# Cross attention: key shares projected two steps ahead and evicted behind both exponentials

## The chip, the cores and the metric

One core of one Trainium2 chip runs the program; the metric is the time of one execution in device microseconds (us). A run is one execution, and the figure of a kernel is the median of its runs.

## The reference, cut to what matters

The program is a two-layer Perceiver-like block on 32 sequences of 64 tokens with 256 channels: cross attention, self attention, a mixture of experts, cross attention again, a two-way Mamba and a feed-forward layer. The change touches only the cross attention, which runs twice:

```python
x = x + xattn(layernorm(x), ctx, ctx, Wq, bq, Wk, bk, Wv, bv, Wo, bo)   # and once more without the biases

# B = 32, 64 queries, 1601 keys with 128 channels, 16 heads of 16
qh = heads(q @ Wq + bq); kh = heads(k @ Wk + bk); vh = heads(v @ Wv + bv)
scores = einsum('bhqd,bhkd->bhqk', qh, kh) * scale
attn = softmax(scores)                     # over the 1601 keys of a sequence
out = einsum('bhqk,bhkd->bhqd', attn, vh)  # then @ Wo + bo
```

## The kernel before, in words

`cross_attention` handles one sequence ("batch") `u` after another. The 1601 keys make 13 tiles of 128, taken in pairs, so a batch has `NG` = 7 steps `g` = 0 to 6 (the last has one tile, of 65 keys), and the two calls have 2 x 224 steps. Every engine has its order of work written out by hand over the same 224 steps, and semaphores tie them together.

**A step on TensorE** (`scores`, then the loop from L597) is, in this order: the scores of the step as keys x queries, in halves called LEAD (heads' strips 0, 1) and TRAIL (2, 3), each closed by `lower` (L560), which subtracts the row maximum with one more matmul; among them four matmuls "M" (`largest`, L481), rounded scores of the *next* batch from which VectorE takes the maxima; then "K" (`project_keys`, L468), one of seven shares of the key projection of a later batch; "V" (`project_values`, L499), the values of step `s + 2`; "P" (`weigh`, L531), the weighted sum of step `s - 1`; at `g` = 6 the transposed maxima "T", at `g` = 1 the sums "S", and at `g` = 3 of every second batch the output projection "W". Before the first score, TensorE waits for both exponentials of the step before, which read the same PSUM tile.

**Banks.** M, K, V, P, T, S and W write into four PSUM banks in rotation (`open_bank`): each waits until the operation four places before it in `ORDER` was read out by its reader (ScalarE for K and V, VectorE for the others). The second M matmul of a step so waits for the eviction of K of the step before.

**ScalarE** (from L642): exponential of LEAD (L650), eviction of K to `kT` (`keep_keys`, L624), exponential of TRAIL, eviction of V (`keep_values`, L632).

**GpSimd** (from L686): rounds the share K just evicted to `kT_hi` (`round_keys`, L674; two buffers), and splits the context of batch `u + 2` into high and low parts for the projections (`split_context`: copy L367, subtraction L369), in three pieces `w` = 0, 1, 2 at `g` = 5, 6 and at `g` = 0 of the next batch. K of share `n` and V wait for the low part of their piece (`raw_lo_done`). GpSimd handles the eviction's rounding first, then the piece, in order.

**VectorE** takes four maxima (L712), adds P to the total (`gather`, L749), and at `g` = 2 divides. **SyncE** loads the context of a batch (L442) once the three pieces of the batch before that in its buffer are split.

At step `(u, g)` the share projected is `(u + 1, g + 1)`, at `g` = 6 `(u + 2, 0)`; the M matmuls of step `(u, g)` read share `(u + 1, g)`, so a share is made one step before it is used. The seventh share, number 6, is small (2 x 65 columns).

Of the kernel before, what the change touches and what calls it, by code (L numbers as in the profile page):

```python
# [13 lines left out]
P = 128  # L14
# [6 lines left out]
NB = 512  # L21
# [240 lines left out]
def cross_attention(nc, tag, x_sb, ident, x_sel, pair_mask, ctxT, wq, wk, wv, wo, bq, bv, bo):  # L262
# [15 lines left out]
    def cols(i):  # L278
# [5 lines left out]
    PROLOGUE = (([("C",)] if bo is not None else []) + [("K", 0, 0)]  # L284
                + [op for n in range(NG) for op in ([("K", 0, n + 1)] if n + 1 < NG else [])
                   + [("M", 0, n, j) for j in range(QUADS)]]
                + [("V", 0), ("V", 1), ("K", 1, 0), ("T", 0)])

    def key_share(u, g):

        return (u + 1, g + 1) if g < NG - 1 else (u + 2, 0)

    LEAD = (0, 1)
    TRAIL = (2, 3)
# [28 lines left out]
    with ExitStack() as ctx:  # L323
# [64 lines left out]
            project_queries(nc, inner, tag, x_sb, ident, qT, wq, bq, loads, split_first)  # L388
        qz = sb(f"{tag}_qz", [P, 2, KD, 2, LQ])
        qz_hi = sb(f"{tag}_qz_hi", [P, 2, KD, 2, LQ], F32R)  # L390
        kT_hi = sb(f"{tag}_kT_hi", [P, 2, NB], F32R)
        kT = sb(f"{tag}_kT", [P, 2, KD, LKV])
        v_sb = sb(f"{tag}_v", [P, NG, 2, H, 2 * DH])
        probs = sb(f"{tag}_probs", [P, 2, QUADS, NB])
# [31 lines left out]
        def last_maximum(b, n):  # L426
            return max((("M", b, n, j) for j in range(QUADS)), key=lambda op: AT[op])

        def made(e, op):

            e.wait_ge(misc_ready, AT[op] + 1)
# [15 lines left out]
        def _(pe):  # L447
# [24 lines left out]
            def largest(op):  # L472
                _, b, n, j = op
                dst = open_bank(op)
                pe.wait_ge(kT_hi_done, b * NG + n + 1)
                if n == 0:
                    pe.wait_ge(qz_hi_done, b + 1)
                rows = slice(j * 32, (j + 1) * 32)
                for m, (c, k0, kn) in enumerate(SHARES[n]):
                    kn += kn % 2  # L480
                    ins = nc.tensor.matmul(dst[:, m * kn:(m + 1) * kn], qz_hi[rows, b % 2, c, :, :].rearrange("p s q -> p (s q)"),  # L481
                                           kT_hi[rows, (b * NG + n) % 2, m * kn:(m + 1) * kn], start=True, stop=True)
                ins.then_inc(misc_ready, 1)

            def turn_maxes(op):
                dst = open_bank(op)
                pe.wait_ge(max_done, op[1] + 1)
                for c in range(KD):
                    ins = nc.tensor.transpose(dst[:, c * P:(c + 1) * P],
                                              neg_max[:, c, :, :].rearrange("p j n -> p (j n)"), ident[:, :])  # L490
                ins.then_inc(misc_ready, 1)
# [45 lines left out]
            def scores(s):  # L537
                u, g = divmod(s, NG)
                mine = tiles(g)
                kn = keys(mine[0])  # L540
                parts = [(h, c) for h in range(len(mine)) for c in range(KD)]
                if g == 0:
                    pe.wait_ge(qz_done, u + 1)
                if s > 0:
                    pe.wait_ge(exp_done, 2 * s)
                if g == 0:
                    read_out(pe, ("T", u))
                last = u + 1 == B

                def score(n, strips):  # L550
                    h, c = parts[n]
                    for j in strips:
                        rows = slice(j * 32, (j + 1) * 32)
                        nc.tensor.matmul(score_ps[0:kn, j, n * P:(n + 1) * P], kT[rows, u % 2, c, cols(mine[h])],  # L554
                                         qz[rows, u % 2, c, :, :].rearrange("p s q -> p (s q)"),
                                         start=n == 0, stop=False, skip_group_check=True)

                def lower(strips):
                    for j in strips:
                        nc.tensor.matmul(  # L560
                            score_ps[0:kn, j, 0:len(mine) * 2 * P], ones[j * 32:j * 32 + 1, 0:kn],
                            shift[j * 32:j * 32 + 1, u % 2, :].rearrange("p (a n) -> p a n", a=1
                                                                         ).broadcast_to([1, len(mine), 2 * P]),
                            start=False, stop=True, skip_group_check=True).then_inc(score_ready[j // 2], 1)

                for n in range(2):
                    score(n, LEAD)
                if not last:
                    for j in TRAIL:
                        largest(("M", u + 1, g, j))  # L570
                for n in range(len(parts)):
                    score(n, TRAIL)
                    if n + 2 < len(parts):
                        score(n + 2, LEAD)
                    elif n + 2 == len(parts):
                        lower(LEAD)
                if not last:
                    for j in LEAD:
                        largest(("M", u + 1, g, j))
                lower(TRAIL)  # L580
# [12 lines left out]
            project_values(("V", 0))  # L593
            project_values(("V", 1))
            project_keys(("K", 1, 0))
            turn_maxes(("T", 0))
            for s in range(STEPS):  # L597
                u, g = divmod(s, NG)
# [17 lines left out]
        @block.scalar  # L616
        def _(act):
            def keep_keys(op):
                _, b, n = op
                made(act, op)  # L620
                c, k0, kn = SHARES[n][0]
                m = len(SHARES[n])
                even = kn + kn % 2
                nc.scalar.activation(kT[:, b % 2, c:c + m, k0:k0 + kn],  # L624
                                     bank(op)[:, 0:m * even].rearrange("p (c k) -> p c k", c=m)[:, :, 0:kn], ACT.Copy
                                     ).then_inc(act_free, 1)

            def keep_values(op):
                g = op[1] % NG
                rows, n = slice(0, keys(tiles(g)[0])), len(tiles(g))  # L630
                made(act, op)
                nc.scalar.activation(  # L632
                    v_sb[rows, g, 0:n, :, 0:DH].rearrange("p a h d -> p (a h) d"),
                    bank(op)[rows, 0:n * D].rearrange("p (a d) -> p a d", d=DH), ACT.Copy).then_inc(act_free, 1)

            act.wait_ge(filled, 1)
            for n in range(NG):
                keep_keys(("K", 0, n))
            keep_values(("V", 0))
            keep_values(("V", 1))  # L640
            keep_keys(("K", 1, 0))
            for s in range(STEPS):  # L642
                u, g = divmod(s, NG)
                rows, n = slice(0, keys(tiles(g)[0])), len(tiles(g)) * 2 * P
                if s > 1:
                    made(act, ("P", s - 2))
                for ph in range(2):
                    js = slice(2 * ph, 2 * ph + 2)
                    act.wait_ge(score_ready[ph], 2 * s + 2)
                    nc.scalar.activation(probs[rows, s % 2, js, 0:n], score_ps[rows, js, 0:n], ACT.Exp).then_inc(exp_done, 1)  # L650
                    if ph == 0 and key_share(u, g)[0] < B:
                        keep_keys(("K",) + key_share(u, g))
                if s + 2 < STEPS:
                    keep_values(("V", s + 2))

        @block.gpsimd
        def _(pool):
# [7 lines left out]
            def round_keys(b, n):  # L665

                at = b * NG + n
                if at > 1:
                    made(pool, last_maximum(*divmod(at - 2, NG)))
                read_out(pool, ("K", b, n))  # L670
                c, k0, kn = SHARES[n][0]
                m = len(SHARES[n])
                even = kn + kn % 2
                nc.gpsimd.tensor_copy(kT_hi[:, at % 2, 0:m * even].rearrange("p (c k) -> p c k", c=m)[:, :, 0:kn],  # L674
                                      kT[:, b % 2, c:c + m, k0:k0 + kn]).then_inc(kT_hi_done, 1)

            pool.wait_ge(w_in, 16 * NW)
# [5 lines left out]
            for b in range(2):  # L683
                queries(b, qz, qz_done)
            round_keys(1, 0)
            for s in range(STEPS):  # L686
                u, g = divmod(s, NG)
                if key_share(u, g)[0] < B:
                    round_keys(*key_share(u, g))
                if g == 0 and 1 < u + 1 < B:  # L690
                    split_context(pool, u + 1, 2)
                if g == 2 and 1 < u + 1 < B:
                    pool.wait_ge(exp_done, 2 * u * NG)
                    queries(u + 1, qz, qz_done)
                if g == 3 and u + 2 < B:
                    made(pool, last_maximum(u, NG - 1))
                    queries(u + 2, qz_hi, qz_hi_done)
                if g == 5 and u + 2 < B:
                    made(pool, ("V", u * NG + NG - 1))
                    split_context(pool, u + 2, 0)  # L700
                if g == 6 and u + 2 < B:
                    split_context(pool, u + 2, 1)

        @block.vector
        def _(dve):
# [1483 lines left out]
```

## Time and profile before

| | |
|---|---|
| median of 3 runs | 4214.39 us (4214.13 to 4221.18) |
| the profiled execution | 4220.17 us, span in the profile 4218.4 us |
| busy share of the span | TensorE matmul 87%, weight load 62%, VectorE 67%, ScalarE 47%, GpSimd 36% |
| load of a batch's context (L442 and the first two), 64 of 800.5 KB | median 4.3 us to landing |

The steps of the first call fill the span from 86 to 1097 us, those of the second from 1929 to 2944 us; what lies between and behind is untouched by the change. A row of a timeline gives the start in us from the span's start, the duration in us, engine, line, operation, tiles, shape and how many instructions were merged; in brackets stands the idle time before it and what ended it.

### The profile page before, as it was taken

What the parts mean: (1) busy time and instruction counts of PE and PEld (TensorE: products, weight loads), DVE (VectorE), ACT (ScalarE), POOL (GpSimd) and SP (SyncE); (2) the same over time, 40 slices, a digit from 0 to 9 for tenths busy, and PEclk for the clock granted to TensorE, in tenths of its full rate; (3) what the DMA queues carried; (4) which work ended last, traced back from release to release, by engine and by line L of the source; (5) the groups of instructions that cost most, each with busy time, mean ns of one, the idle gap of its engine ahead of it and who ended that gap; (6) DMA issues with size and microseconds to landing.
All of it is one profiled execution on the core that took longest, in us unless ns stands there. A gap on an engine that the chain in (4) does not pass through costs nothing. (4 is left out here: it accounts for less than half of the span.)

```text
span 4218.4 us, 129595 instructions
## 1 busy us (share of the span) xinstructions
PE 3654.6 (87%) x54334; PEld 2636.2 (62%) x54335; DVE 2813.2 (67%) x4793; ACT 1986.8 (47%) x2986; POOL 1523.2 (36%) x1445
## 2 busy tenths in 40 slices
PE   6999999999797299939999999999778778787888
PEld 4888888888687266627888888887323333332357
DVE  5667667666466122236666666665979999999964
ACT  2666666666333122205666666665444444444432
POOL 3333333333000200042333333332067777788710
PEclk8999999999898599968999999999889998999989
DMA  2000001000001501020000100100022222222200
GB/s 64 27 30 31 27 27 34 27 27 19 9 0 56 208 28 32 30 79 25 27 27 27 34 27 27 34 27 3 27 67 70 70 69 71 73 78 73 70 29 20
DMA packets 79936, 182.53 MB, mean 43 GB/s; under 512 B 10754, under 2 KB 31266, under 8 KB 79042
## 3 DMA queue, kind: packets, MB, share of 16 engines
q1 hardware_dynamic: 76354, 166.58, 12.7%
q8 instruction: 413, 6.77, 0.7%
q0 software_dynamic: 3072, 8.39, 0.6%
q14 instruction: 97, 0.79, 0.1%
HBM read 157.37 MB, written 17.56 MB: 41 GB/s over the span
## 5 line engine op out<-in xcount | busy, mean ns | idle before, releaser
L650 ACT ACTIVATE x_probs<-x_score_ps 128x1024 f32<-128x1024 f32 (+1 forms) x896 | 861.0, 963 | 648.3 <-PE x_score_ps L560 641.3
L712 DVE TENSOR_REDUCE x_maxes<-x_misc_ps 128x1 f32<-128x512 f32 (+1 forms) x1792 | 1010.4, 626 | 145.6 <-PE x_misc_ps L481 145.2
L674 POOL CAST x_kT_hi<-x_kT 128x512 fp32r<-128x512 f32 (+1 forms) x448 | 259.5, 579 | 1360.6 <-PE x_misc_ps L499 836.8
L1706 PE MATMUL b_acc_ps<-b_read,ident 128*128 128x512 f32 x1024 | 564.9, 681 | 190.5 <-POOL b_read L1792 157.0
L1784 POOL TENSOR_TENSOR b_drive<-b_b_all,b_dtx 128x1024 f32<-128x1024 f32 x256 | 603.1, 2357 | 331.1 <-DVE b_dtx L1864 281.1
L554 PE MATMUL x_score_ps<-x_qz,x_kT 32*128 32x128 f32 x13312 | 641.0, 277 | 43.3 <-ACT x_probs L650 38.3
L554 PEld LDWEIGHTS x_score_ps<-x_qz,x_kT 32*128 32x128 f32 x13312 | 551.6, 182 | 117.3 <-ACT x_probs L650 60.5
L1826 DVE TENSOR_TENSOR_SCAN b_state<-b_decay_ps,b_drive 128x512 f32<-128x512 f32 x512 | 607.0, 1205 | 12.5 <-POOL b_drive L1784 12.5
L1774 ACT ACTIVATE b_decay_ps<-b_dt,b_a_neg 128x504 f32<-128x504 f32 x512 | 350.0, 685 | 461.9 <-DVE b_state L1826 461.9
L1706 PEld LDWEIGHTS b_acc_ps<-b_read,ident 128*128 128x128 f32 x1024 | 193.8, 211 | 507.7 <-POOL b_read L1792 260.1
L531 PE MATMUL x_misc_ps<-x_probs,x_v 128*32 128x64 f32 x26624 | 464.6, 221 | 0.5 <-issue 0.5
L481 PE MATMUL x_misc_ps<-x_kT_hi,x_qz_hi 32*128 32x512 f32 (+1 forms) x2048 | 452.9, 403 | 5.0 <-POOL x_kT_hi L674 3.0
L531 PEld LDWEIGHTS x_misc_ps<-x_probs,x_v 128*32 128x32 f32 x26624 | 392.3, 110 | 66.4 <-issue 18.2
L749 DVE TENSOR_TENSOR x_u<-x_misc_ps,x_u 128x256 f32<-128x256 f32 x384 | 162.5, 423 | 308.7 <-PE x_misc_ps L531 308.6
L560 PE MATMUL x_score_ps<-x_shift,x_ones 1*128 1x512 f32 (+1 forms) x1792 | 367.1, 459 | 0.3 <-issue 0.3
L624 ACT ACTIVATE x_kT<-x_misc_ps 128x512 f32<-128x512 f32 (+1 forms) x448 | 248.2, 554 | 207.0 <-PE x_misc_ps L468 194.1
L632 ACT ACTIVATE x_v<-x_misc_ps 128x512 f32<-128x512 f32 (+1 forms) x448 | 255.9, 571 | 12.4 <-PE x_misc_ps L499 12.3
L1836 DVE TENSOR_TENSOR b_read<-b_c_ps,b_state 128x512 f32<-128x512 f32 x384 | 254.0, 661 | 0.0
L468 PE MATMUL x_misc_ps<-x_raw_hi,x_wk_hi 128*128 128x512 f32 (+1 forms) x512 | 230.9, 451 | 24.0 <-POOL x_v L680 8.9
L481 PEld LDWEIGHTS x_misc_ps<-x_kT_hi,x_qz_hi 32*128 32x128 f32 x2048 | 235.5, 186 | 24.7 <-DVE x_u L749 8.8
L499 PE MATMUL x_misc_ps<-x_wv_hi,x_raw_hi 128*128 128x256 f32 (+1 forms) x832 | 241.3, 290 | 0.1
L369 POOL TENSOR_TENSOR x_raw_lo<-x_raw,x_raw_hi 128x512 fp32r<-128x512 f32 (+1 forms) x192 | 235.3, 1225 | 15.5
(282 smaller groups left out, 5816.1 us busy)
## 6 DMA issues: line engine op xcount, KB each, us to landing
x_raw<-in_ctxT SPq DMA_DIRECT2D x64, 800.5 KB, 4.3
b_b_all<-b_bc_rows SPq DMA_DIRECT2D x128, 256.0 KB, 3.5
b_c_all<-b_bc_rows SPq DMA_DIRECT2D x128, 256.0 KB, 3.2
m_w<-in_m_w SPq DMA_DIRECT2D x16, 704.0 KB, 19.1
m_w<-in_m_w SPq DMA_DIRECT2D x8, 768.0 KB, 19.6
m_slot_rows<-m_zero SPq DMA_DIRECT2D x1, 4992.0 KB, 17.1
m_block_rows<-m_slot_rows SPq DMA_DIRECT2D x39, 128.0 KB, 2.0
m_slot_out<-m_out SPq DMA_DIRECT2D x39, 128.0 KB, 1.7
```

What stands on the lines that cost most here:

```text
L481: ins = nc.tensor.matmul(dst[:, m * kn:(m + 1) * kn], qz_hi[rows, b % 2, c, :, :].rearrange("p s q -> p (s q)"), kT_hi[rows, (b * NG + n) ...
L531: ins = nc.tensor.matmul(dst[j * 32:(j + 1) * 32, r * LQ:(r + 1) * LQ], v_sb[0:keys(i), g, h, 8 * c + 2 * j + half, :], probs[0:keys(i), s ...
L554: nc.tensor.matmul(score_ps[0:kn, j, n * P:(n + 1) * P], kT[rows, u % 2, c, cols(mine[h])], qz[rows, u % 2, c, :, :].rearrange("p s q -> p ...
L560: nc.tensor.matmul(score_ps[0:kn, j, 0:len(mine) * 2 * P], ones[j * 32:j * 32 + 1, 0:kn], shift[j * 32:j * 32 + 1, u % 2, :].rearrange("p ...
L632: nc.scalar.activation(v_sb[rows, g, 0:n, :, 0:DH].rearrange("p a h d -> p (a h) d"), bank(op)[rows, 0:n * D].rearrange("p (a d) -> p a d" ...
L650: nc.scalar.activation(probs[rows, s % 2, js, 0:n], score_ps[rows, js, 0:n], ACT.Exp).then_inc(exp_done, 1)
L674: nc.gpsimd.tensor_copy(kT_hi[:, at % 2, 0:m * even].rearrange("p (c k) -> p c k", c=m)[:, :, 0:kn], kT[:, b % 2, c:c + m, k0:k0 + kn]).th ...
L712: nc.vector.tensor_reduce(maxes[:, c:c + m, j, k0 // NB], bank(op)[:, 0:m * even].rearrange("p (c k) -> p c k", c=m)[:, :, 0:kn], AX.X, AL ...
L1706: nc.tensor.matmul(acc_ps[:, c, :], ident[:, :], read[:, c, :], start=False, stop=True, skip_group_check=True).then_inc(acc_done, 1)
L1774: nc.scalar.activation(by_sequence(decay_ps[:, c % 2, :])[:, :, inside(p)], by_sequence(dt[:, c, :])[:, :, inside(p)], ACT.Exp, scale=a_ne ...
L1784: nc.gpsimd.tensor_tensor(drive[:, c:c + 2, :], b_all[:, k % 2:k % 2 + 1, :].broadcast_to([P, 2, NB]), dtx[:, c:c + 2, :], ALU.mult).then_ ...
L1826: nc.vector.tensor_tensor_scan(order(state[:, c, :]), order(decay_ps[:, c % 2, :]), order(drive[:, c, :]), 0.0, ALU.mult, ALU.add).then_in ...
```

## The change

- The share of step `(u, g)` becomes `(u + 1, g + 2)`, at `g` = 5 and 6 `(u + 2, 0)` and `(u + 2, 1)`; one more share is made ahead of the loop. `kT_hi` gets a third buffer.
- ScalarE evicts K behind both exponentials.
- TensorE waits for the first exponential alone ahead of the LEAD scores, and for the second ahead of the TRAIL scores.
- GpSimd splits the pieces `w` = 0, 1, 2 at `g` = 4, 5, 6, each one step earlier.

```diff
-                + [("V", 0), ("V", 1), ("K", 1, 0), ("T", 0)])
+                + [("V", 0), ("V", 1), ("K", 1, 0), ("K", 1, 1), ("T", 0)])
     def key_share(u, g):
-        return (u + 1, g + 1) if g < NG - 1 else (u + 2, 0)
+        return (u + 1 + (g + 2) // NG, (g + 2) % NG)
...
-        kT_hi = sb(f"{tag}_kT_hi", [P, 2, NB], F32R)
+        kT_hi = sb(f"{tag}_kT_hi", [P, 3, NB], F32R)
...
-                                           kT_hi[rows, (b * NG + n) % 2, m * kn:(m + 1) * kn], start=True, stop=True)
+                                           kT_hi[rows, (b * NG + n) % 3, m * kn:(m + 1) * kn], start=True, stop=True)
...
                 if s > 0:
-                    pe.wait_ge(exp_done, 2 * s)
+                    pe.wait_ge(exp_done, 2 * s - 1)
...
                 if not last:
                     for j in TRAIL:
                         largest(("M", u + 1, g, j))
+                if s > 0:
+                    pe.wait_ge(exp_done, 2 * s)
                 for n in range(len(parts)):
                     score(n, TRAIL)
...
             project_keys(("K", 1, 0))
+            project_keys(("K", 1, 1))
...
             keep_keys(("K", 1, 0))
+            keep_keys(("K", 1, 1))
...
-                    if ph == 0 and key_share(u, g)[0] < B:
-                        keep_keys(("K",) + key_share(u, g))
+                if key_share(u, g)[0] < B:
+                    keep_keys(("K",) + key_share(u, g))
                 if s + 2 < STEPS:
                     keep_values(("V", s + 2))
...
-                if at > 1:
-                    made(pool, last_maximum(*divmod(at - 2, NG)))
+                if at > 2:
+                    made(pool, last_maximum(*divmod(at - 3, NG)))
...
             round_keys(1, 0)
+            round_keys(1, 1)
             for s in range(STEPS):
                 u, g = divmod(s, NG)
                 if key_share(u, g)[0] < B:
                     round_keys(*key_share(u, g))
-                if g == 0 and 1 < u + 1 < B:
-                    split_context(pool, u + 1, 2)
...
-                if g == 5 and u + 2 < B:
-                    made(pool, ("V", u * NG + NG - 1))
-                    split_context(pool, u + 2, 0)
-                if g == 6 and u + 2 < B:
-                    split_context(pool, u + 2, 1)
+                w = g - (NG - WIDE)
+                if w >= 0 and u + 2 < B:
+                    made(pool, ("V", u * NG + (2 * w + 1 if w < WIDE - 1 else NG - 1)))
+                    split_context(pool, u + 2, w)
```

## Rows read from the trace of the kernel before

**Rows 1.** Busy time by stretch: the first call's steps (columns in the first line)
```profile
core 0: us, PE busy (x) PEld busy (x) DVE busy (x) ACT busy (x) POOL busy (x), PEclk, DMA share, GB/s
86.00:1097.00 1011.00, 982.49 (x24046) 821.07 (x24047) 682.04 (x1261) 628.58 (x887) 320.93 (x457) 1.00 0.08 26
```

**Rows 2.** Waits: who waited for what, us in total, times, longest
```profile
PEld x_misc_ps L468 <- DVE x_maxes L712: 120.0, 425, 0.8
...
PEld x_score_ps L554 <- ACT x_probs L650: 60.5, 135, 1.1
```

**Rows 3.** The tile of the low context part: who waited for it, us, times
```profile
  PE x_misc_ps L468: 6.0, 31
```

**Rows 4.** Timeline of PE, batch 10 from its step 2, into batch 11
```profile
413.93 0.50 PE L468 MATMUL x_misc_ps<-x_raw_hi,x_wk_hi 128*128 128x512 f32 x1
...
415.52 1.10 PE L531 MATMUL x_misc_ps<-x_probs,x_v 128*32 128x64 f32 x64
416.55 0.38 PE L554 MATMUL x_score_ps<-x_qz,x_kT 32*128 32x128 f32 x2
...
423.26 0.38 PE L554 MATMUL x_score_ps<-x_qz,x_kT 32*128 32x128 f32 x2
...
424.84 0.50 PE L468 MATMUL x_misc_ps<-x_raw_hi,x_wk_hi 128*128 128x512 f32 x1
...
426.08 1.10 PE L531 MATMUL x_misc_ps<-x_probs,x_v 128*32 128x64 f32 x64
427.40 0.38 PE L554 MATMUL x_score_ps<-x_qz,x_kT 32*128 32x128 f32 x2 [0.22 <-ACT x_probs L650]
...
429.17 0.30 PE L468 MATMUL x_misc_ps<-x_raw_hi,x_wk_hi 128*128 128x66 f32 x1
...
431.78 0.33 PE L554 MATMUL x_score_ps<-x_qz,x_kT 32*65 32x128 f32 x2
...
432.84 0.50 PE L468 MATMUL x_misc_ps<-x_raw_hi,x_wk_hi 128*128 128x512 f32 x1
...
435.71 0.38 PE L554 MATMUL x_score_ps<-x_qz,x_kT 32*128 32x128 f32 x2
...
438.89 0.65 PE L531 MATMUL x_misc_ps<-x_probs,x_v 65*32 65x64 f32 x32
439.85 0.38 PE L554 MATMUL x_score_ps<-x_qz,x_kT 32*128 32x128 f32 x2 [0.31 <-ACT x_probs L650]
...
441.89 0.47 PE L468 MATMUL x_misc_ps<-x_raw_hi,x_wk_hi 128*128 128x512 f32 x1 [0.20 <-POOL x_raw_lo L369]
```

**Rows 5.** Timeline of ACT: steps 4, 5, 6 of batch 10; then the last batch
```profile
424.77 1.02 ACT L650 ACTIVATE x_probs<-x_score_ps 128x1024 f32<-128x1024 f32 x1 [3.07 <-PE x_score_ps L560]
...
430.06 0.28 ACT L624 ACTIVATE x_kT<-x_misc_ps 128x130 f32<-128x130 f32 x1
...
433.85 0.60 ACT L624 ACTIVATE x_kT<-x_misc_ps 128x512 f32<-128x512 f32 x1 [0.56 <-PE x_misc_ps L468]
...
1078.39 1.94 ACT L650 ACTIVATE x_probs<-x_score_ps 128x1024 f32<-128x1024 f32 x2 [1.08 <-PE x_score_ps L560]
1080.21 0.60 ACT L632 ACTIVATE x_v<-x_misc_ps 128x512 f32<-128x512 f32 x1
```

**Rows 6.** Timeline of POOL: the low parts of one batch, and one piece of another
```profile
431.42 1.27 POOL L369 TENSOR_TENSOR x_raw_lo<-x_raw,x_raw_hi 128x512 fp32r<-128x512 f32 x1
...
435.83 1.28 POOL L369 TENSOR_TENSOR x_raw_lo<-x_raw,x_raw_hi 128x512 fp32r<-128x512 f32 x1
...
440.33 1.42 POOL L369 TENSOR_TENSOR x_raw_lo<-x_raw,x_raw_hi 128x577 fp32r<-128x577 f32 x1
...
590.98 1.09 POOL L369 TENSOR_TENSOR x_raw_lo<-x_raw,x_raw_hi 128x512 fp32r<-128x512 f32 x1
```

**Rows 7.** Timeline of PE in the last batch, step 1
```profile
1076.87 1.16 PE L554 MATMUL x_score_ps<-x_qz,x_kT 32*128 32x128 f32 x30 [0.51 <-ACT x_probs L650]
...
1079.21 1.10 PE L531 MATMUL x_misc_ps<-x_probs,x_v 128*32 128x64 f32 x64
```

More of the change, by code:

```diff
@@ L673, in round_keys @@
                 even = kn + kn % 2
-                nc.gpsimd.tensor_copy(kT_hi[:, at % 2, 0:m * even].rearrange("p (c k) -> p c k", c=m)[:, :, 0:kn],
+                nc.gpsimd.tensor_copy(kT_hi[:, at % 3, 0:m * even].rearrange("p (c k) -> p c k", c=m)[:, :, 0:kn],
                                       kT[:, b % 2, c:c + m, k0:k0 + kn]).then_inc(kT_hi_done, 1)
```

## The prediction, made before the change was run

> **What bounds the kernel now.** I read the busy times by stretch first. In the steps of a call TensorE's matmul rows are busy 982.49 of 1011 us at a granted clock of 1.00 (2.4 GHz), ScalarE 629, VectorE 682, GpSimd 321 [rows 1]: TensorE's queue sets the pace, and another engine costs time only where that queue stands still for it. The waits say where it does. Over both calls it is 120.0 us, in 425 steps, ahead of K for VectorE's maxima, which the change leaves alone, and 60.5 us, 135 times, at the first score for the exponentials, which is the change's target [rows 2]. For GpSimd's low context parts the matmuls stood only 6.0 us, 31 times [rows 3].
>
> The timeline shows these waits in single steps. Where nothing waits, the next step's first score starts 1.03 us behind the start of P (415.52 to 416.55), 0.07 before P's end [rows 4]. Step 4 of batch 10 has P at 426.08, so step 5 could start at 427.11; it starts at 427.40, late by 0.29, released by the exponential. Step 0 of batch 11 has its short P at 438.89, ends it at 439.54, could hand over at 439.47, and does at 439.85: late by 0.38. In the other steps P ends last. So a batch holds some 0.67 us of this wait in two steps, and 62 batches some 42 us of the 60.5.
>
> **The chain that I follow.** GpSimd rounds the evicted keys, then splits a context piece, and K of the next step needs that piece. The pieces move one step earlier, and so do the shares that read them: the distance between them stays one step. But GpSimd's step begins with the key eviction, and that moves behind the second exponential. All times below are from the start of the named step.
>
> *ScalarE.* The first exponential starts 1.51 in (424.77 less 423.26) [rows 4, 5]. Two exponentials back to back hold the next instruction back by 1.82 (1078.39 to 1080.21) [rows 5], so the eviction starts at 3.33. Before, the small one in step 5 started at 2.66 (430.06 less 427.40). By the Trainium skill (ScalarE: Activation LUTs, section What ACT_TABLE_LOAD costs) an activation of N elements takes 186 ns plus 0.833 ns each and back-to-back ones overlap by about 93 ns. That is an estimate of 0.95 us of spacing where the trace has 0.91, and by it each late piece below would be 0.07 later, some 8 us in all.
>
> *Step 4, now with the small share.* Its length loses the 0.29 and nothing else, since a small K and a large one take alike from K to the next step (429.17 to 431.78 is 2.61, 413.93 to 416.55 is 2.62 [rows 4]): 3.85. From the small eviction to the subtraction's start is 1.36 (430.06 to 431.42), the subtraction takes 1.27, in alternate batches 1.09 [rows 5, 6], and K follows its end by 0.15 (432.69 to 432.84; 441.75 to 441.89) [rows 4, 6]. The piece so lets K go at 3.33 + 1.36 + 1.27 + 0.15 = 6.11, or 5.93. K of step 5 would want to go at 3.85 + 1.58 = 5.43 (1.58 is 424.84 less 423.26). **It stands 0.68 or 0.50 us.** Step 6 starts 2.62 later, at 8.73 or 8.55, where before it started at 8.52.
>
> *Step 5.* Its eviction starts at 3.85 + 3.33 = 7.18. A full share has 1.98 from eviction to subtraction (433.85 to 435.83) [rows 5, 6]: K of step 6 can go at 7.18 + 1.98 + 1.28 + 0.15 = 10.59, or 10.40. It would want to at 8.73 + 1.06 = 9.79 or 9.61 (432.84 less 431.78) [rows 4]. **It stands 0.80 us.** From there to the next batch is 2.87 (432.84 to 435.71): 13.46 or 13.27, against 12.45 before (423.26 to 435.71). These three steps lose 1.01 or 0.82.
>
> *Step 6.* Its K is late, so its eviction comes 1.01 behind that K (432.84 to 433.85). I estimate the subtraction of the widest piece to start 2.04 behind it, 0.06 more than for a full one, and take it at 1.42, or some 0.2 less [rows 6]. K of step 0 can go 1.01 + 2.04 + 1.42 + 0.15 = 4.62 (or 4.4) behind the late K, and would want to at 2.87 + 1.58 = 4.45: late by 0.17, or not at all.
>
> *Steps 0 and 1.* The wait of 0.38 goes; with the 0.17 that leaves 0.21 in alternate batches. What is late next is the bank: the second M matmul of step 1 waits for the eviction of step 0, which now ends at 3.33 + 0.60 = 3.93. With 0.05 for the release, an estimate below GpSimd's 0.15, I put M at 3.98, where it would want to go near 3.78: 0.2 lost in one kind of batch, little in the other. Before, K of step 1 went at 2.04 in batch 11 (441.89 less 439.85), held by the widest piece, and I estimate 1.84 where the pieces are 0.2 shorter. Now it goes at 1.58 plus what M lost. So step 1 gains some 0.40 in the batches with long pieces and 0.05 in the others.
>
> *The sum.* Long pieces: +1.01 - 0.21 - 0.40 = +0.40. Short pieces: +0.82 - 0.38 - 0.05 = +0.39. I take +0.395 for each of the 60 batches whose steps split a piece (30 in a call): +23.7 us. The next to last batch splits nothing and gains some 0.5; the last one has no M and no K, and both exponentials end last there: those from 1078.39 end at 1080.33 and would let go at 1080.38, P from 1079.21 would hand over at 1080.24 [rows 5, 7]. That is 0.14 in each of five steps, and the first, with its short P, has near the whole 0.51 of idle time: some 1.2. Twice 1.7 is -3.4. Together **+20 us**.
>
> *Costed at nothing.* The extra share ahead of the loop is taken from step 6 of the next to last batch. The third buffer only loosens a wait. The new wait ahead of the TRAIL scores holds those and all behind them, but its exponential ends at 1.51 + 0.91 + 1.02 = 3.44, before any next step starts. The context load of SyncE is released one step earlier with the widest piece, takes 4.3 us, and is needed four steps later. Rounding has two steps for its share instead of one. If GpSimd's pieces were not late, these covers would still stand.
>
> The profiled execution took 4220.17 us, 5.8 above the median of 4214.39. From it I get 4240; as a median of runs, 4214.4 + 20 = **4234**.
>
> **Rivals.**
> *Faster: the pieces come in time.* Place: the K of steps 5 and 6. It decides at 5.43 after the start of step 4: were the low part done by 5.28, nothing would stand. For it speaks that GpSimd is idle two thirds of the time [rows 1] and that it did just this before [rows 3]. Against it, GpSimd's queue is in order with the eviction at its head, and the sum misses by 0.50 at least. Then the three steps take 3.85 + 4.20 + 3.93 = 11.98 instead of 12.45, and a batch gains 0.47 + 0.38 + 0.15 = 1.00: 60 times, with the 3.4, -63 us, 4151. By the Trainium skill (Perfetto Trace Analysis, section Identifying the Most-Contended Engine) TensorE's headroom is judged by its weight loads, here 821 of 1011 us or 81% [rows 1]. That would leave it room to gain from every wait removed; the waits for exponentials in the trace are 60.5 us in all [rows 2].
> *No difference.* The late pieces cost what the exponentials give: one of the two stands, say the 0.80 halved. A batch then breaks even: about 4214.
> *Slower by more.* The bank wait of M in step 1 also takes the overlap of M with the scores. Step 5 began behind a wait and had its K at 1.77 instead of 1.58 [rows 4]. If step 1 does so in each batch, 0.19 x 60 is 11 more, and 4245; with longer subtractions when they lie beside the moved eviction, 4256.
> *The change doesn't do what it says*: the first scores can't start earlier, since P sits before them. That is so in five steps of seven already; its chance is counted with the case of no difference.
>
> **How the numbers follow.** Forecast (4222 to 4245) 0.50; faster by the pieces in time or mostly so 0.20; no difference 0.15; slower by more 0.15. Within 0.2% (8.4 us, about what a measurement can tell) falls 0.18 and above it 0.62 (0.03 of the forecast lies within). The range from 4185 to 4256 takes in the break-even and half of the way to the faster case, and leaves the full -63 out. Its bounds cover the subtraction of 1.09 to 1.28 and the skipped 0.2 of M.
>
> **What would show it.** Right: the wait of the first score for the exponential is nearly gone; K's wait for the low part rises from 6 us to some 70 to 90; step 4 shrinks to 3.85, steps 5 and 6 take 4.7 to 4.9; the key eviction starts at 3.33. Wrong: K in step 5 before 5.9 from the start of step 4, or no wait for L369; then the faster case holds. M in step 1 at 3.8 would show no bank wait.

## The result and the profile after

The changed kernel takes 4227.42 us (median of 9 runs, 4224.98 to 4230.58), the kernel before 4215.44 us in the same comparison. The ratio is 1.0028, 95% interval 1.0017 to 1.0038: slower by 12.0 us. The forecast was 4234, slower by 20.

The profiled execution took 4226.03 us, with a span of 4224.3. The busy times of the first call's steps (columns as in [rows 1]), which now end at 1101 instead of 1097 us:

```profile
86.00:1101.00 1015.00, 966.38 (x24015) 806.13 (x24013) 686.82 (x1260) 615.10 (x886) 317.72 (x455) 1.00 0.08 26
```

TensorE's matmul rows fell from 982.49 to 966.38 us while the stretch grew by 4: TensorE stands idle for longer. The granted clock is 1.00 as before. The waits of the changed kernel (who waited for what, us in total, times, longest) say for what:

```profile
PEld x_misc_ps L468 <- DVE x_maxes L714: 190.4, 407, 1.1
...
PE x_misc_ps L468 <- POOL x_raw_lo L369: 67.6, 93, 1.1
...
PEld x_score_ps L554 <- ACT x_probs L654: 0.6, 2, 0.3
```

The wait of the first score for an exponential is gone, 60.5 to 0.6 us [rows 2]. In its place K waits for the low context parts, 67.6 us where it was 6.0 [rows 3]. The row above it, up from 120.0 to 190.4 [rows 2], is partly the same wait: K waits for VectorE's maximum and for the low part in one place, and the profile books the idle time of the weight loads to one name and that of the matmuls to the other. The run e1 below decides it: with the low parts in time the 190.4 fall to 103.6.

The timeline of PE shows the steps 4, 5 and 6 of batch 12, one of those whose pieces take GpSimd 1.27 us ("long", against 1.09):

```profile
488.29 0.38 PE L554 MATMUL x_score_ps<-x_qz,x_kT 32*128 32x128 f32 x2
...
489.87 0.30 PE L468 MATMUL x_misc_ps<-x_raw_hi,x_wk_hi 128*128 128x66 f32 x1
...
492.06 0.38 PE L554 MATMUL x_score_ps<-x_qz,x_kT 32*128 32x128 f32 x2
...
494.39 0.47 PE L468 MATMUL x_misc_ps<-x_raw_hi,x_wk_hi 128*128 128x512 f32 x1 [0.68 <-POOL x_raw_lo L369]
...
497.00 0.33 PE L554 MATMUL x_score_ps<-x_qz,x_kT 32*65 32x128 f32 x2
...
498.80 0.48 PE L468 MATMUL x_misc_ps<-x_raw_hi,x_wk_hi 128*128 128x512 f32 x1 [0.78 <-POOL x_raw_lo L369]
...
501.62 0.38 PE L554 MATMUL x_score_ps<-x_qz,x_kT 32*128 32x128 f32 x2
```

Timelines of ACT and of POOL in the same steps:

```profile
489.81 1.94 ACT L654 ACTIVATE x_probs<-x_score_ps 128x1024 f32<-128x1024 f32 x2 [3.77 <-PE x_score_ps L560]
491.63 0.29 ACT L627 ACTIVATE x_kT<-x_misc_ps 128x130 f32<-128x130 f32 x1
```
```profile
492.05 0.29 POOL L678 CAST x_kT_hi<-x_kT 128x130 fp32r<-128x130 f32 x1 [5.38 <-ACT x_kT L627]
492.28 0.61 POOL L367 CAST x_raw_hi<-x_raw 128x512 fp32r<-128x512 f32 x1
492.98 1.27 POOL L369 TENSOR_TENSOR x_raw_lo<-x_raw,x_raw_hi 128x512 fp32r<-128x512 f32 x1
...
497.38 1.27 POOL L369 TENSOR_TENSOR x_raw_lo<-x_raw,x_raw_hi 128x512 fp32r<-128x512 f32 x1
```

Read as one chain: the exponentials start 1.52 after the step and hold the eviction until 3.34 (491.63). GpSimd, idle for 5.38 us, rounds and only then splits, the low part is done at 494.25, and K follows at 494.39, which is 6.10 after the start of step 4. Step 4 is 3.77 long, step 5 4.94, step 6 4.62: 13.33 together, where they were 12.45 [rows 4].

Step 1 shows the wait for the bank. The timeline of PE at the start of the steps 0 and 1 of the same batch has the second M matmul of step 1 at 472.40, 0.24 behind the start of its step:

```profile
468.40 0.38 PE L554 MATMUL x_score_ps<-x_qz,x_kT 32*128 32x128 f32 x2
...
472.16 0.38 PE L554 MATMUL x_score_ps<-x_qz,x_kT 32*128 32x128 f32 x2
472.18 0.49 PE L481 MATMUL x_misc_ps<-x_kT_hi,x_qz_hi 32*128 32x512 f32 x1
...
472.40 0.50 PE L481 MATMUL x_misc_ps<-x_kT_hi,x_qz_hi 32*128 32x512 f32 x1
```

The key eviction of step 0, which that bank waits for, ends at 472.35 (timeline of ACT):

```profile
471.74 0.61 ACT L627 ACTIVATE x_kT<-x_misc_ps 128x512 f32<-128x512 f32 x1
```

One step is longer and was not on the list, step 3: 6.89 us in the even batches, which project the output there, where it was 6.71, and in the odd ones 4.95 where it was 4.77. Its K starts 2.34 after the step's start (483.74), before it was 2.16. VectorE's division in step 2 is the way to the cause. The group of its product (L733 before, L735 now), first the row of the kernel before, then that of the changed one; columns busy us and mean ns, then the idle time before it:

```profile
L733 DVE TENSOR_TENSOR x_oT<-x_u,x_recip 128x256 f32<-128x256 f32 x64 | 27.2, 424 | 2.2
```
```profile
L735 DVE TENSOR_TENSOR x_oT<-x_u,x_recip 128x256 f32<-128x256 f32 x64 | 37.9, 592 | 2.2
```

The same instruction takes 0.17 us more in each batch. Timelines of POOL and DVE of the changed kernel, step 2 of batch 12:

```profile
481.86 0.61 POOL L663 TENSOR_TENSOR x_qz<-x_qT,x_mask 128x256 f32<-128x256 f32 x1
```
```profile
482.15 0.60 DVE L735 TENSOR_TENSOR x_oT<-x_u,x_recip 128x256 f32<-128x256 f32 x1
482.67 0.41 DVE L751 TENSOR_TENSOR x_u<-x_misc_ps,x_u 128x256 f32<-128x256 f32 x1
```

GpSimd's masked queries now lie beside the product. In the same step of the kernel before (timelines of POOL and DVE) they had ended before the product began:

```profile
480.40 0.63 POOL L659 TENSOR_TENSOR x_qz<-x_qT,x_mask 128x256 f32<-128x256 f32 x1
```
```profile
481.47 0.42 DVE L733 TENSOR_TENSOR x_oT<-x_u,x_recip 128x256 f32<-128x256 f32 x1
```

They started 3.88 us into their step and now start 4.65 into it: moving the key eviction moved them 0.8 us later. Behind the product stands `gather` (L751), which frees the bank that an M matmul of step 3 waits for, and behind that one stands K.

### The profile page after: what moved, and what is told of

It reads as the page before. It is cut to its first block and busy times, and to the rows that moved or that the text cites. A ratio compares the mean times of both kernels' runs of the same rounds, so it can differ in the third digit from the quotient of the medians.

```text
span 4224.3 us, 129713 instructions
## 1 busy us (share of the span) xinstructions
PE 3622.3 (86%) x54334; PEld 2605.3 (62%) x54335; DVE 2823.5 (67%) x4793; ACT 1962.3 (46%) x2986; POOL 1518.5 (36%) x1445
## 5 line engine op out<-in xcount | busy, mean ns | idle before, releaser
L654 ACT ACTIVATE x_probs<-x_score_ps 128x1024 f32<-128x1024 f32 (+1 forms) x896 | 814.3, 960 | 739.0 <-PE x_score_ps L560 729.8
L554 PE MATMUL x_score_ps<-x_qz,x_kT 32*128 32x128 f32 x13312 | 614.5, 277 | 1.4 <-DVE x_shift L724 1.2
L554 PEld LDWEIGHTS x_score_ps<-x_qz,x_kT 32*128 32x128 f32 x13312 | 525.1, 182 | 65.4 <-issue 32.1
L751 DVE TENSOR_TENSOR x_u<-x_misc_ps,x_u 128x256 f32<-128x256 f32 x384 | 162.2, 422 | 321.6 <-PE x_misc_ps L531 321.6
L560 PE MATMUL x_score_ps<-x_shift,x_ones 1*128 1x512 f32 (+1 forms) x1792 | 348.4, 458 | 0.3 <-issue 0.3
L468 PE MATMUL x_misc_ps<-x_raw_hi,x_wk_hi 128*128 128x512 f32 (+1 forms) x512 | 227.5, 444 | 99.3 <-POOL x_raw_lo L369 67.6
L481 PEld LDWEIGHTS x_misc_ps<-x_kT_hi,x_qz_hi 32*128 32x128 f32 x2048 | 216.5, 186 | 45.5 <-DVE x_u L751 29.7
L369 POOL TENSOR_TENSOR x_raw_lo<-x_raw,x_raw_hi 128x512 fp32r<-128x512 f32 (+1 forms) x192 | 234.6, 1222 | 15.5
```

Of the source, the lines that this page charges most:

```text
L560: nc.tensor.matmul(score_ps[0:kn, j, 0:len(mine) * 2 * P], ones[j * 32:j * 32 + 1, 0:kn], shift[j * 32:j * 32 + 1, u % 2, :].rearrange("p ...
```

## The experiments

e1 to e4 are edits of the changed kernel and share the runs of the kernel before (4215.08 us).

**e1: the split ahead of the rounding.**

```diff
 for s in range(STEPS):
     u, g = divmod(s, NG)
+    w = g - (NG - WIDE)
+    if w >= 0 and u + 2 < B:
+        made(pool, ("V", u * NG + (2 * w + 1 if w < WIDE - 1 else NG - 1)))
+        split_context(pool, u + 2, w)
     if key_share(u, g)[0] < B:
         round_keys(*key_share(u, g))
...
-    w = g - (NG - WIDE)
...
-        split_context(pool, u + 2, w)
```

> Edit to the changed kernel: GpSimd splits the context piece ahead of rounding the share, so the split no longer stands behind the key eviction. Theory 1 (the pieces are late only because the eviction is ahead of them in GpSimd's queue): the low part is done some 3 us before K wants it, K of steps 5, 6 and 0 stops waiting for it (67.6 us in the profile of the changed kernel falls to about 0), step 5 goes from 4.94 or 4.73 to 4.20, step 6 from 4.63 to about 3.9, and a batch loses 1.46 or 1.27: about -82 us against 4227, so 4145, ratio to the kernel before 0.983. Rival (GpSimd's own speed, or another wait behind it, holds K): steps 5 and 6 stay above 4.5 and the time above 4200.

Measured: 4149.38 us, ratio 0.9842 (0.9827 to 0.9857). Timeline of PE in the same three steps of batch 12:

```profile
479.67 0.38 PE L554 MATMUL x_score_ps<-x_qz,x_kT 32*128 32x128 f32 x2
...
481.26 0.50 PE L468 MATMUL x_misc_ps<-x_raw_hi,x_wk_hi 128*128 128x512 f32 x1
...
483.88 0.33 PE L554 MATMUL x_score_ps<-x_qz,x_kT 32*65 32x128 f32 x2
...
484.94 0.50 PE L468 MATMUL x_misc_ps<-x_raw_hi,x_wk_hi 128*128 128x512 f32 x1
...
487.81 0.38 PE L554 MATMUL x_score_ps<-x_qz,x_kT 32*128 32x128 f32 x2
```

Step 5 is 4.21 long, step 6 3.93, and no K waits for L369 any more: that row is gone from the waits. The low part for K of step 5 was done at 476.17, before its step began:

```profile
474.90 1.27 POOL L369 TENSOR_TENSOR x_raw_lo<-x_raw,x_raw_hi 128x512 fp32r<-128x512 f32 x1
```

GpSimd does the same work at the same speed; only its order changed. The place in the queue made the pieces late, and the lateness cost 78 us.

**e2: the queries one step earlier.**

```diff
-                if g == 2 and 1 < u + 1 < B:
+                if g == 1 and 1 < u + 1 < B:
                     pool.wait_ge(exp_done, 2 * u * NG)
                     queries(u + 1, qz, qz_done)
```

> Edit to the changed kernel: GpSimd makes the masked queries of the next batch at step 1 instead of step 2. Theory 2 (in step 2 the moved GpSimd work lies beside VectorE's product of two SBUF operands, L735, which takes 0.60 instead of 0.42 us, and its delay passes through gather and the bank of M to K of step 3): the product is back at 0.42, K of step 3 goes from 2.32 back to 2.15 after the step's start, -0.18 in each of 62 batches, -11 us: about 4216, ratio 1.000. Rival (step 3 is longer for another reason, such as the longer steps before): K of step 3 stays at 2.32 and the time at 4227.

Measured: 4215.26 us, ratio 0.9999 (0.9990 to 1.0008). From the timelines of POOL, DVE and PE, batch 12:

```profile
476.90 0.61 POOL L663 TENSOR_TENSOR x_qz<-x_qT,x_mask 128x256 f32<-128x256 f32 x1
```
```profile
482.22 0.42 DVE L735 TENSOR_TENSOR x_oT<-x_u,x_recip 128x256 f32<-128x256 f32 x1
```
```profile
481.48 0.38 PE L554 MATMUL x_score_ps<-x_qz,x_kT 32*128 32x128 f32 x2
...
483.63 0.50 PE L468 MATMUL x_misc_ps<-x_raw_hi,x_wk_hi 128*128 128x512 f32 x1
```

The product is back at 0.42 and K of step 3 at 2.15. The 12 us are as large as the whole loss of the change: without this overlap the change would have come out even.

**e3: both.**

> Both edits together. If theories 1 and 2 are both right and independent, the gains add: 4227 - 82 - 11 = 4134, ratio 0.981. If the pieces, now early in GpSimd's step, lie beside VectorE's work and slow it, less: 4145 or above.

Measured: 4139.29 us, ratio 0.9819 (0.9804 to 0.9834). The two gains add: 88 us against 78 + 12 = 90.

**e4: the wait for both exponentials back ahead of the first score.**

```diff
-                    pe.wait_ge(exp_done, 2 * s - 1)
+                    pe.wait_ge(exp_done, 2 * s)
```

> Edit to the changed kernel: TensorE waits for both exponentials ahead of the first score again. Theory 3 (the halved wait is worth nothing where P sits before the scores, since with the eviction behind them both exponentials end 3.46 after the step's start and the next step starts at 3.75 at the earliest): steps 0 to 6 stay as they are, and only the steps of the last batch and the first step of the first, now 2.9 to 3.4 long, go back to 3.51, some 1.5 us a call: about 4230, ratio 1.0035. Rival (the halved wait is what removes the wait at steps 0 and 4): these go back up by 0.3 to 0.4 each, +40 us, 4267.

Measured: 4228.97 us, ratio 1.0034 (1.0022 to 1.0046), where the changed kernel has 1.0028. In the changed kernel the halved wait is worth nothing that can be told: the moved eviction alone lets the exponentials end before P. In the traces only the edges of a call show it: the last batch takes 21.57 us from the start of its first step to that of its last, where the changed kernel takes 20.03.

e5 to e8 share 4216.38 us of the kernel before; e5 to e7 are edits of that kernel.

**e5: the halved wait alone.** As in the change, `2 * s - 1` ahead of the first score and `2 * s` ahead of the TRAIL scores.

> Edit to the kernel before: the halved wait alone (first exponential ahead of the LEAD scores, second ahead of the TRAIL scores); eviction, shares and splits as before. Theory 3 goes on: with the eviction between them the second exponential ends 4.10 after the step's start, and the TRAIL scores want to start near 3.95, so the wait of 0.38 at step 0 shrinks to some 0.2. K of step 1 is held by the widest context piece anyway (it goes at 5.97 or 6.18 after the start of step 0), so nothing comes of it there; step 4 may give 0.1 to 0.3. 62 times that, and some 2 in the last batches: -8 to -20 us, about 4202, ratio 0.997. Rival (the halved wait removes both waits in full): -0.67 x 62 = -42, 4173, ratio 0.990.

Measured: 4194.86 us, ratio 0.9953 (0.9939 to 0.9967). That is a little beyond the expected range. This one part of the change is a gain by itself. Its trace places it in step 4, which goes from 4.15 to 3.86 us (even batches, medians). At step 0 the whole wait goes, 4.14 to 3.76, and not half of it as expected, but step 1 loses as much, 5.06 to 5.43: its K is held by the widest context piece and goes 5.96 us after the start of step 0 either way.

**e6: the eviction alone.**

```diff
-                    if ph == 0 and key_share(u, g)[0] < B:
-                        keep_keys(("K",) + key_share(u, g))
+                if key_share(u, g)[0] < B:
+                    keep_keys(("K",) + key_share(u, g))
```

> Edit to the kernel before: the key eviction moved behind both exponentials, nothing else. GpSimd's rounding then starts 4.08 after the step's start and ends at 4.69, and the first M of the next step, which reads it, can go at 4.84 instead of 3.8 to 4.2: three steps of a batch lose 1.0, 0.6 and 1.0, and the late context pieces some 1.3 more, less the 1.2 of waits that the eviction removes: about +168 us, 4380, ratio 1.04. That would show why the shares had to go two steps ahead. Rival (rounding has slack enough in its one step): the time stays within 20 us of the kernel before.

Measured: 4352.83 us (one run), 136 above the kernel before, where 168 were expected. Timeline of PE in a step 1, with the M matmuls 1.08 behind the step's start:

```profile
499.09 0.71 PE L554 MATMUL x_score_ps<-x_qz,x_kT 32*128 32x128 f32 x8
500.17 0.59 PE L481 MATMUL x_misc_ps<-x_kT_hi,x_qz_hi 32*128 32x512 f32 x2 [0.37 <-POOL x_kT_hi L674]
```

M waits for the rounding of its keys, and this is what the second step of lead was needed for. How much of the 136 is this wait and how much the context pieces, which the moved eviction makes late here too, no run separates.

**e7: the split ahead of the rounding, in the kernel before.**

> Edit to the kernel before: GpSimd splits the context piece ahead of rounding the share, at the steps of before. The control for e1: is the gain there that of the order alone? Theory: before, only K of step 1 waited for a piece (at 2.04 or 1.83 after the step's start; behind the exponential's wait it would go at 1.77), and step 6 a little, so the order is worth 0.27 or 0.06 a batch: -10 us, 4205, ratio 0.9976. The 66 us of e1 beyond that then need the change. Rival (the order alone is the gain): 4150, ratio 0.984.

Measured: 4206.22 us, ratio 0.9976 (0.9967 to 0.9985). The order alone is worth 10 us there and 78 in the changed kernel, so what e1 repaired is for the most part a loss that the change had made.

**e8: e3 with the eviction back between the exponentials.** The edit of e6 reversed.

> Edit to e3 (both GpSimd edits on the changed kernel): the key eviction goes back between the two exponentials. Is the moved eviction needed once the pieces are early? Theory: with shares two steps ahead and the halved wait, the second exponential ends at 4.10 and only the TRAIL scores of step 1 want it before (near 3.95), where now the second M stands as long for the bank of the eviction; steps 2 to 6 end with P. So it is about the same as e3: 4139 to 4145, ratio 0.982 to 0.9835. Rival (the moved eviction is what removes the waits at steps 0 and 4): 0.67 x 62 = +42 us, 4181, ratio 0.992.

Measured: 4143.82 us, ratio 0.9833 (0.9820 to 0.9847). Its interval overlaps that of e3: no gain of the moved eviction can be told once the pieces are early. The medians differ by 4 us, and the typical batch is alike in the two traces, 31.6 us in the even and 29.7 in the odd ones.

**e9: the halved wait of e5 and the order of e7, without the second step of lead. e10: e3 again beside it.** Both share 4215.80 us.

> Edit to the kernel before: the halved wait of e5 and GpSimd's order of e7 together, shares one step ahead and the eviction between the exponentials as before. What is the shares' second step worth once the pieces are early? Theory: steps 0 and 1 come to the 8.8 of e8 (they take 9.2 to 9.4 in e5, where the widest piece holds K), steps 4 and 5 stay at the 8.3 of e5, where the TRAIL scores of step 5 wait for the second exponential, against 8.0 in e8, where the small share of step 4 lets it start earlier: 0.33 a batch above e8, +20 us, 4164, ratio 0.988. Rival (the second step adds nothing): as e3, 4140, ratio 0.982. Second rival (the two edits do not add): as e5, 4195, ratio 0.995.

> e3 again, on the same chip as e9, with more rounds: the best version so far, for a direct comparison. 4139, ratio 0.982; if e9's rival is right, the two are the same.

Measured: e9 4173.99 us, ratio 0.9899 (0.9884 to 0.9914); e10 4139.16 us, ratio 0.9821 (0.9807 to 0.9834). So the version of e3 is 35 us faster than e9, and the expectation for e9 was 10 too low. The two edits together give 42, more than their sum of 32, since in step 1 K is then held by neither: it goes 1.95 us after the start of that step in e9, at 2.20 or 2.40 in e5. The missing 10 stand in step 1 of e9, 5.21 long against 4.97 in e8. Timelines of POOL and PE, start of a step 1:

```profile
462.52 0.61 POOL L676 CAST x_kT_hi<-x_kT 128x512 fp32r<-128x512 f32 x1 [1.91 <-PE x_misc_ps L499]
```
```profile
462.97 0.49 PE L554 MATMUL x_score_ps<-x_qz,x_kT 32*128 32x128 f32 x4
463.28 0.46 PE L481 MATMUL x_misc_ps<-x_kT_hi,x_qz_hi 32*128 32x512 f32 x1
```

The step starts at 462.97, but its first M reads the keys whose rounding ends at 463.13, and goes at 463.28. Of the readings of e9 this one is argued from the two rows alone; no run took that wait away by itself. With shares two steps ahead (e8) the keys are rounded a step earlier, and that M goes 0.03 behind the start of its step.

| Version | us | against before |
|---|---|---|
| the change | 4227.4 | +12.0 |
| the change, queries at step 1 (e2) | 4215.3 | +0.2 |
| the change, split first (e1) | 4149.4 | -65.7 |
| the change with both (e3, e10) | 4139.3, 4139.2 | -75.8, -76.6 |
| e3 with the eviction back between (e8) | 4143.8 | -72.6 |
| the change, wait for both (e4) | 4229.0 | +13.9 |
| before, halved wait (e5) | 4194.9 | -21.5 |
| before, split first (e7) | 4206.2 | -10.2 |
| before, both (e9) | 4174.0 | -41.8 |
| before, eviction alone (e6, one run) | 4352.8 | +136 |

## Why the prediction was right, and where it was off

**The bound and the wait removed: right.** TensorE's queue stayed the pace, and the exponential's wait vanished.

**The chain that makes the pieces late: right, term by term.** The eviction was put at 3.33 and is at 3.34; K of step 5 at 6.11 and is at 6.10; step 4 at 3.85 and is 3.77; three steps at 13.46 and are 13.33 (K of step 6 stands 1.80 - 1.06 = 0.74 instead of 0.80, and the way from it to the next batch takes 2.82 instead of 2.87). e1 shows the cause: with the order turned, both waits are gone and so are 78 us. Two exponentials again hold the next instruction back by 1.82 (489.81 to 491.63), 0.91 each. The estimate by the Trainium skill (ScalarE: Activation LUTs, section What ACT_TABLE_LOAD costs) is 0.95 each; the measurement decides against it.

**The bank of M in step 1: right.** Eviction of step 0 until 3.95, M at 4.00 (472.40 less 468.40) against 3.98 forecast. The release took 0.05, as estimated. K of step 1 went 1.80 or 1.66 us after the start of its step, which is the 1.58 plus what M lost.

**Step 3, left out of the sum: wrong.** The prediction costed GpSimd's rounding at nothing and named what waits for it, but not what follows it in GpSimd's queue: the masked queries of step 2. Moved 0.8 us later, they lie beside the product and lengthen step 3 by 0.18 us in each batch, some 11 us in all. e2 shows it at 12. No rival had it either.

**The size, +20 against +12, with two terms that went the other way.** Per batch the sum had +0.40 for long pieces and +0.39 for short ones. From the starts of the batches in the two traces, batch 12 took 32.55 and takes 33.22 us (long pieces), +0.67, and batch 3 took 31.01 and takes 31.13 (short ones), +0.12. The long one's is 0.88 in steps 4 to 6 and 0.18 in step 3, less 0.39 in step 0. The mean is +0.395, as forecast, but that is luck, by errors that cancel. Step 3 was missing (+0.18 in every batch). Against it, the short batches' steps 4 to 6 were measured against a long one's 12.45, while their own before was 12.57, and in both kinds these steps came out some 0.13 shorter than in the sum (for a long one 13.33 instead of 13.46). So 58 typical batches, those that split and are not first, give the +22.9 expected of them.

The term that was mis-sized is that of the ends: -3.4 in the sum. The first batch, counted as a loser, gained (30.43 to 29.32 us, in the second call 31.01 to 29.33): its step 0 has no P, so that before the change the exponentials alone set its length, and it fell from 4.69 to 3.37, in the second call from 4.65. The next to last gained 1.45 and 1.73 instead of 0.5. The share that is now made ahead of the loop is missing from its step 5, which fell from 4.38 to 3.51, and not from its step 6 as the prediction has it. The last batch, up to its sums, gained 1.13 and 0.91 against 1.2. That is 8.0 us instead of 2.6 (the forecast's 3.4 less the 0.8 that it had charged to the first batches). 22.9 - 8.0 is +14.9, and the 2.9 that are left to the measured +12.0 lie within the interval, which reaches from +7 to +16 us.

A sum over typical batches is not the sum over all. In the two traces the 58 batches grew by 15.2 us only (925.0 to 933.9 us in the first call, 927.5 to 933.8 in the second), since the trace of the kernel before has more single batches that are longer than their like. One of them is longer by 3.3 us, and in it TensorE stood 2.0 us for nothing that the profile names. With the ends that is +7.2, near the 5.9 by which the two spans differ; the medians of the runs differ by 12.0. What makes single batches long stays open.

**The rivals.** "Faster: the pieces come in time" was priced at -63 and is e1: -66. Its mechanism was right, its condition not met. That the price fits is in part luck: e1 still has the loss of step 3 in it, and without that (e3) it is -76. "No difference" would have been the time without the overlap of step 2 (e2), but not by its mechanism: in e2 both K stand as long as in the changed kernel (steps 5 and 6 are 4.93 and 4.64). "Slower by more", by 0.19 in K of step 1, did not happen: K went where the forecast had it. That the halved wait changes nothing in most steps holds inside the change (e4), not in the kernel before (e5): there the exponentials end last at steps 0 and 4, and the first of the two is enough to start the next step.

By the Trainium skill (Perfetto Trace Analysis, section Identifying the Most-Contended Engine) headroom is read from the busy share of the weight loads, here 81% before, and from the share of peak FLOPs. The trace agrees as far as e3 goes: the steps gave up some 77 us of waits with the same matmuls. The row alone didn't say which waits.

## What to carry to other kernels

When an operation moves later on one engine, follow it through the next engine's queue and price everything that stands behind it there, not only its direct reader: here a key eviction moved by some 0.8 us, its reader had slack, and the two things behind the reader did not. If work with an early deadline stands behind work with slack, turn the order first; that made the same change worth -66 us instead of +12, and -76 with the masked queries moved as well. Then ask again whether the move is needed at all: here, with the order turned and the queries moved, no difference could be told with the eviction back in its old place (e8).

## What the runs showed of the hardware

A VectorE product of two SBUF operands (128x256, float) took 0.42 us by itself and 0.60 us beside a GpSimd product that reads SBUF; in the mean of 64 of them it was 424 and 592 ns, and e2, which moved the GpSimd work away, has 425. By the Trainium skill (SBUF - State Buffer, section Who interferes with whom) a VectorE instruction with two SBUF inputs contends with a GpSimd instruction that reads SBUF, for a shared pair of ports that the section calls an exclusive lock. The trace agrees that they contend. The size is below that of a lock held to GpSimd's end: with the product starting at 482.15 and GpSimd ending at 482.47, it would have ended at 482.89, and it ended at 482.75. GpSimd's spans in the profile are rough, so how much of that difference is real stays open.

The subtraction L369 takes 1.09 us in batches of one parity and 1.27 in the others, before and after, in e1 as well, where it lies elsewhere in the step. The two kinds of batch use the two halves of the same buffers; why these differ stays open.
